# A selective-scan kernel: the scan laid out by channel instead of by channel and state, with a different hand-over between VectorE and GpSimd

## The reference

```python
x_proj = x @ in_proj_w.T + in_proj_b              # 256 -> 512: x_ssm and x_gate
x_conv = silu(depthwise_conv4(x_ssm) + conv_b)
B, C   = split(x_conv @ bc_w.T + bc_b)            # 16 states each, per token
dt     = softplus(x_conv @ dt_w.T + dt_b)         # per token and channel
A      = -exp(A_log)                              # 256 channels x 16 states
h      = h * exp(dt * A) + (dt * B) * x_conv      # scan over 512 tokens
y      = sum_n(h * C) + x_conv * D
z      = (y * silu(x_gate)) @ out_w.T + out_b + x
x1     = layernorm(x + layernorm(z) * ln_g + ln_b)
# experts: top 4 of 8 per token, softmax weights, gated unit of width 512
out    = layernorm(x1 + experts(x1))
```

## Time and profile before

| | us |
|---|---|
| median of 3 runs (1518.12 to 1525.36) | 1522.14 |
| profiled execution, its own time | 1521.88 |
| span of that execution | 1520.1 |
| start of the first scan | 57.6 |
| start of the last scan | 726.3 |
| DVE busy | 1157.5 |
| PE busy | 1073.6 |
| ACT busy | 853.5 |
| POOL busy | 796.4 |

### The profile page before, as it was taken

The page is one execution under the profiler, slowest core; times in us unless marked ns, Lnnn a source line. Parts: engine busy times, 40 slices in busy tenths (PEclk is TensorE's granted clock), DMA queues, the critical chain, the costliest instruction groups (busy, mean ns, idle before and its releaser), DMA issues. The chain is left out here.

```text
span 1520.1 us, 18561 instructions
## 1 busy us (share of the span) xinstructions
PE 1073.6 (71%) x5074; PEld 737.0 (48%) x5074; DVE 1157.5 (76%) x1665; ACT 853.5 (56%) x1353; POOL 796.4 (52%) x519
## 2 busy tenths in 40 slices
PE   6455657383755737351516999999999999999960
PEld 2111222131312213020215888888888888888850
DVE  1688999999998999999444677777777766777753
ACT  2564646455444645532114677777767766777744
POOL 0245557767676776778770444444444444444452
PEclk9786868596876859655557999999999999999995
DMA  1899998888988889786274555666566555565637
GB/s 65 210 275 265 234 273 227 255 253 224 264 243 238 235 253 245 212 265 190 80 258 180 148 147 152 162 166 165 149 150 150 148 150 149 147 155 155 166 62 225
DMA packets 137418, 292.22 MB, mean 192 GB/s; under 512 B 14880, under 2 KB 50464, under 8 KB 132640
## 3 DMA queue, kind: packets, MB, share of 16 engines
q1 hardware_dynamic: 97824, 242.48, 53.1%
q0 software_dynamic: 26880, 36.72, 14.6%
q10 hardware_dynamic: 12672, 12.58, 2.6%
HBM read 232.71 MB, written 59.02 MB: 192 GB/s over the span
## 5 line engine op out<-in xcount | busy, mean ns | idle before, releaser
L956 POOL TENSOR_TENSOR read<-state,c_rep 128x1024 f32<-128x1024 f32 x128 | 301.6, 2357 | 254.1 <-DVE state L796 249.5
L796 DVE TENSOR_TENSOR_SCAN state<-decay,p_bu 128x1024 f32<-128x1024 f32 x128 | 292.3, 2283 | 9.5 <-ACT decay L637 3.5
L1370 POOL DMA_INDIRECT total<-o_v,tok x144 | 267.6, 1858 | 44.1 <-issue 44.0
L637 ACT ACTIVATE decay<-first_wl,scan_rate 128x511 f32<-128x511 f32 x192 | 127.9, 713 | 256.4 <-DVE state L796 227.3
L484 PE MATMUL p_y<-read,small 128*32 128x512 f32 x512 | 96.4, 836 | 217.4 <-POOL read L956 217.4
L1368 POOL TENSOR_TENSOR scrap<-neg_half 128x1 f32<-128x1 f32 x36 | 13.9, 385 | 355.9 <-ACT o_v L1255 353.5
L1232 ACT ACTIVATE gate_v<-p_g,bias 128x512 f32<-128x512 f32 x144 | 98.5, 684 | 97.4 <-PE p_up L1181 97.3
L787 DVE TENSOR_TENSOR p_bu<-first_wh,p_b 128x1024 f32<-128x1024 f32 x96 | 118.0, 1229 | 30.9 <-DMA first_wh<-scan_in 16.2
L484 PEld LDWEIGHTS p_y<-read,small 128*32 128x32 f32 x512 | 11.5, 124 | 267.8 <-POOL read L956 258.1
L1242 ACT ACTIVATE ah<-a_v 128x512 fp32r<-128x512 f32 x144 | 91.2, 633 | 88.2 <-DVE a_v L1316 88.2
L1305 DVE TENSOR_SCALAR up_v<-up_v 128x512 f32<-128x512 f32 x144 | 61.3, 425 | 64.2 <-ACT up_v L1235 64.1
(11 more groups left out here) (200 smaller groups left out, 3017.6 us busy)
## 6 DMA issues: line engine op xcount, KB each, us to landing
first_wl<-scan_in SPq DMA_DIRECT2D x192, 256.0 KB, 4.7
first_wh<-scan_in SPq DMA_DIRECT2D x192, 256.0 KB, 5.7
first_raw<-in_w_experts SPq DMA_DIRECT2D x19, 1668.0 KB, 6.8
raw_w<-in_w_experts SPq DMA_DIRECT2D x18, 1668.0 KB, 6.8
dt_rep<-scan_in SPq DMA_DIRECT2D x64, 256.0 KB, 4.9
u_rep<-scan_in SPq DMA_DIRECT2D x64, 256.0 KB, 5.6
first_rows<-queues SPq DMA_DIRECT2D x19, 544.0 KB, 6.9
xq<-queues SPq DMA_DIRECT2D x18, 544.0 KB, 6.9
```

Of the source, the lines that this page charges most:

```text
L637: act.activation(decay[t % 2][:, i, 1:LEN], dt_rep[t % RING][:, i, 1:LEN], ACT.Exp, scale=rate[:, g:g + 1])\
L796: dve.tensor_tensor_scan(flat(state[t % 4][:, :, :]), flat(decay[t % 2][:, :, :]), p_bu[:, :], 0.0, ALU.mult, ALU.add).then_inc(s_state, 1)
L956: pool.tensor_tensor(read[quad % 2][:, tiles[0]:tiles[0] + 2, :], state[t % 4][:, :, :], c_rep[s.p][:, :].unsqueeze(1).broadcast_to([P, 2, ...
L1370: pool.indirect_dma_start(total, bass.IndirectOffsetOnAxis(ap=tok[t.p][:, a:a + 1], axis=0), o_v[t.p][:, a, :], None, compute_op=ALU.add). ...
```

## The change

- A slot is now one state n of all 256 channels: partition = channel, the two halves of 512 elements are channels 0 to 127 and 128 to 255. `dt` and `u` need no replication: `decays` reads `dt` from SBUF and `u` lies in a PSUM tile `p_u`. Instead B and C (32 rows of 512) go to DRAM and come back spread over all partitions, 1 MB for each two slots (`replicate`); one DMA where there were eight.
- `sum_states` is now, in each slot, two matmuls of 128 columns with the identity as weights, accumulating over 16 slots; the D term is two more matmuls with a diagonal matrix (`skip_w`), in place of `skip_path`. Both halves of `p_y` are one accumulation; the next sequence's starts when `gate` has read it (`s_y`).
- The gate reads PSUM in two instructions, in slot 2 behind the ranking.
- Softplus: two DVE instructions instead of three, one more on ACT, moved to slot 11; dt in slot 13, u in slot 15.
- POOL's read of slot t-1 waits for the product of slot t (`s_bu`), and in slots 2, 5, 11, 12, 13, 15 for the side work named below. The scatters of a slot all stand ahead of that read. The offset of x moves to slot 3; the output bias has `ln_b` taken off and is added by a bfloat16 matmul of three rows.
- The first loads are split: what the input projection needs comes first. The order of A_log and of its biases is set up by small matmuls (`order_rate`, `place_rate`).

```diff
+        def sum_states(s, t):
+            n = SLOTS * s.n + t
+            if t == 0:
+                after(pe, s_y, s.n)
+                for h in range(HALVES):
+                    pe.matmul(p_y[h][:, :], skip_w[:, h, :], xc[s.p][:, h, :], start=True, stop=False)
+            pe.wait_ge(s_read, n + 1)
+            for h in range(HALVES):
+                mm = pe.matmul(p_y[h][:, :], ident[:, :], read[:, t % 4, h, :], start=False, stop=(t == SLOTS - 1))
+            mm.then_inc(s_added, 1)
...
         for r in rounds(pe):
             for t in range(SLOTS):
-                if t in (0, 2) and r.c:
-                    sum_states(r.s.at(-1), QUADS - 2 + t // 2)
-                if t >= 4 and t % 2 == 0 and r.b:
-                    sum_states(r.s, t // 2 - 2)
+                if t < 2 and r.c:
+                    sum_states(r.s.at(-1), SLOTS - 2 + t)
...
                 if r.a and t == 8:
+                    from_xc(r, "bc", BC, 2 * STATE)
...
+                if t >= 2 and r.b:
+                    sum_states(r.s, t - 2)
...
         def softplus(r):
             act.activation(flat(expo[:, :, :]), flat(expo[:, :, :]), ACT.Exp, scale=-1.0).then_inc(s_exp, 1)
+            if r.like == Round.FIRST:
+                rate_exp()
+            act.activation(flat(rest[:, :, :]), flat(expo[:, :, :]), ACT.Identity, bias=1.0).then_inc(s_t, 1)
             act.activation(flat(logp[:, :, :]), flat(expo[:, :, :]), ACT.Ln, bias=1.0).then_inc(s_log, 1)
...
         def decays(s, t):
             after(act, s_state, SLOTS * s.n + t - 1)
+            for h in range(HALVES):
+                act.activation(decay[t % 2][:, h, 1:LEN], dt[s.p][:, h, 1:LEN], ACT.Exp, scale=rate[:, h, t:t + 1])\
                    .then_inc(s_decay, 1)
...
         def softplus_rest(r):
+            dve.wait_ge(s_t, s.n + 1)
+            dve.scalar_tensor_tensor(flat(rest[:, :, :]), flat(rest[:, :, :]), -1.0, flat(expo[:, :, :]),
+                                     ALU.add, ALU.subtract).then_inc(s_rest, 1)
             dve.wait_ge(s_log, s.n + 1)
             dve.tensor_tensor(flat(relu[:, :, :]), flat(relu[:, :, :]), flat(logp[:, :, :]), ALU.add).then_inc(s_sum, 1)
+        def drive(r):
+            after(dve, s_bu, SLOTS * s.n)
+            dve.tensor_tensor(p_u[:, :], flat(dt[s.p][:, :, :]), flat(xc[s.p][:, :, :]), ALU.mult).then_inc(s_u, 1)
...
         def read_state(s, t):
             n = SLOTS * s.n + t
             pool.wait_ge(s_state, n + 1)
+            after(pool, s_added, n - 3)
+            pool.tensor_tensor(read[:, t % 4, :, :], state[t % 4][:, :, :], of_state(t, 1), ALU.mult).then_inc(s_read, 1)
...
+        SCATTERS = {6: (0,), 7: (1,), 8: (2,), 10: (3, 4), 13: (5, 6), 14: (7,), 15: (8,)}
+        def while_scanning(r, t):
+            pool.wait_ge(s_bu, SLOTS * r.s.n + t + 1)
+            if r.d and t == 2:
+                pool.wait_ge(s_rexp, 2 * r.s.at(-2).n + 1)
+            if r.d and t == 5:
+                pool.wait_ge(s_index, r.s.at(-2).n + 1)
+            if r.a and t == 11:
+                pool.wait_ge(s_sum, r.s.at(1).n + 1)
+            if r.c and t == 12:
+                pool.wait_ge(s_residual, r.s.at(-1).n + 1)
+            if r.a and t == 13:
+                pool.wait_ge(s_dt, r.s.at(1).n + 1)
+            if r.a and t == 15:
+                pool.wait_ge(s_u, r.s.at(1).n + 1)
...
+        def replicate(s, pair):
+            if pair == 0:
+                sp.wait_ge(s_put[s.p], 16 * (s.use + 1))
+            after(sp, s_read, SLOTS * s.n + 2 * (pair - RING + 1))
+            rows_of = bc_rows[s.p, 2 * pair:2 * pair + 2, :, :]
+            sp.dma_start(bc[pair % RING][:, :, :, :], rows_of.unsqueeze(0).broadcast_to([P, 2, 2, LEN]))\
+              .then_inc(s_rep[pair % RING], 16)
```

More of the change, by code:

```diff
@@ L72, in blocks @@
         return (["tr0", "tr1", "rt"] * d + ["in0", "in1", "cv0"] * a + ["cnt"] * d + ["cv1"] * a + ["o0", "o1"] * c
-                + ["dt0", "dt1", "bb", "cc", "in2", "in3"] * a)
+                + ["bc", "dt0", "dt1", "in2", "in3"] * a)
     def block(self, name):
[L77 to L80, removed]
+        start = sum(len(Round(Seq(0, i), i).blocks()) for i in range(Round.FIRST, self.like))
+        k = start + self.blocks().index(name)
+        turns = 0 if isinstance(self.s.half, int) else self.s.half - Round.LOOP.start // 2
+        return k % 2, k // 2 + 1 + len(self.blocks()) * turns
 def rounds(eng):
@@ L469, in convolve, with from_xc @@
                 mm.then_inc(bank_full[b], 1)
-        def from_xc(r, name, weight):
+        def from_xc(r, name, at, n):
             bank, done = block(r, name)
-            if name == "dt0":
+            if name == "bc":
                 pe.wait_ge(s_silu, 2 * r.s.at(1).n + 1)
[L475 to L486, removed]
+            product(bank[0:n, :], columns(at, n), lambda k: xc[r.s.at(1).p][:, k, :]).then_inc(done, 1)
+        def sum_states(s, t):
[5 more added lines that the diff above has]
+            pe.wait_ge(s_read, n + 1)
+            for h in range(HALVES):
+                mm = pe.matmul(p_y[h][:, :], ident[:, :], read[:, t % 4, h, :], start=False, stop=(t == SLOTS - 1))
+            mm.then_inc(s_added, 1)
         def project_out(r, b):
@@ L555, in pe_stage1, with rate_rows, rate_exp @@
                     project_out(r, t - 6)
+                if r.like == Round.FIRST and t == 5:
+                    order_rate()
                 if r.a and t == 8:
+                    from_xc(r, "bc", BC, 2 * STATE)
                     for i in range(HALVES):
-                        from_xc(r, f"dt{i}", columns(DT_ + i * P, P))
+                        from_xc(r, f"dt{i}", DT_ + i * P, P)
                 if r.like == Round.FIRST and t == 9:
[L560 to L563, removed]
+                    place_rate()
                 if r.a and t in (10, 11):
                     project(r, t - 8)
+                if t >= 2 and r.b:
+                    if t == 2 and r.like == 0:
+                        pe.wait_ge(s_set_dve, SET_DVE)
+                    sum_states(r.s, t - 2)
     def act_stage1(act):
[L569 to L572, removed]
+        act.wait_ge(s_first, FIRST_SETUP)
+        def rate_rows():
+            act.wait_ge(s_order, 1)
+            for h in range(HALVES):
+                last = act.activation(rate_t[0:STATE, h, :], p_y[h][0:STATE, 0:P], ACT.Copy)
+            last.then_inc(s_set_act, 1)
+        def rate_exp():
+            act.wait_ge(s_order, 2)
+            act.activation(flat(rate[:, :, :]), p_u[:, 0:GROUPS], ACT.Exp).then_inc(s_set_act, 1)
         def store_in(r, m):
@@ L706, in act_stage1 @@
                     store_conv(r, 0)
+                if r.like == Round.FIRST and t == 6:
+                    rate_rows()
                 if r.a and t == 8:
+                    store_bc(r)
                     store_dt(r, 0)
                     store_dt(r, 1)
[L710 to L712 removed]
                 if r.c and t == 9:
@@ L934, in dve_stage1 @@
                     weave(moments(r.s.at(-1), 0))
-                if r.a and t == 10:
+                if r.a and t == (11 if r.b else 10):
                     softplus_rest(r)
-                if r.b and t == 11:
-                    skip_path(r.s, 0)
-                if r.a and t == 11:
+                if r.like == Round.FIRST and t == 11:
+                    negate_rate(dve)
+                if r.a and t == 13:
                     scan_inputs(r)
@@ L942, in dve_stage1 @@
                     residual(r)
+                if r.a and t == SLOTS - 1:
+                    drive(r)
                 if r.b:
@@ L1000, in pool_stage1 @@
             for t in range(SLOTS):
-                if r.d and t in SCATTERS_BEFORE:
-                    scatter(r.s.at(-2), SCATTERS_BEFORE[t])
+                if r.d and t in SCATTERS:
+                    scatter(r.s.at(-2), SCATTERS[t])
+                if r.e and t < 7:
+                    scatter(r.s.at(-3), range(t + 9, t + 10))
+                if r.b:
+                    while_scanning(r, t)
                 if t == 0 and r.c:
```

245 lines of the change are left out of this document (121 added, 124 removed).

## The result

The changed kernel took 1471.99 us (median of 4, 1469.88 to 1474.04) against 1520.13 for the kernel before on the same chip (four executions too): a ratio of 0.968, 95% interval 0.965 to 0.971. The profiled execution took 1474.04 us with a span of 1472.2. I had said 1496.

The account below looks back on a forecast made before the run. VectorE was taken to bound stage 1. Steady rounds -13 us, rounds 0 and 1 -9, round 7 -6, start -2, tail +4: -26 from 1521.9, so 1496 us; own range 1480 to 1514, 8 in 10 1455 to 1545.

Parts of the forecast that it names:

- What bounds it: Stage 1: VectorE bounds, busy 72.4 of 76 us; a microsecond off its instructions is worth one until another engine is late.
- Instructions removed and waits inside durations: VectorE's side work in a steady round: removed instructions and waits for GpSimd recorded as duration, together -7.1 us.
- New wait (1), TensorE before the ranking: Slots 0 to 2: VectorE waits for the logits behind TensorE's sums, 0 to 4 us a round, taken 1.5.
- rival A: PE and ACT keep pace and neither new wait shows: -59 us in all, 1463 us; chance 0.22.
- rival B: PE becomes the bound, where its mean instruction costs over 0.62 us: slower, 1545 us; chance 0.20.
- New wait (2), the decay of slot 10: Slot 10's scan waits for ScalarE's decay, wanted 3.7 us earlier: 0 to 5 us a round, taken 3.
- Rounds 0 and 1: First two rounds of stage 1, without ranking: together 143 us for 152.5, so -9.
- Start: Before the first scan: projection some 4 us earlier, but `place_rate` ahead of the fourth projection; -6 to +3, taken -2.
- Round 7: Last round, without softplus: D term 1.5, ranking 0.7, residual -4.4, wait +0.6, in all -6 us.
- Tail: After the last scan: gate behind ranking, router behind sum 15, 6 to 9 us later, less 2.5 and 2: +4.
- The form of softplus: Softplus's `scalar_tensor_tensor` with two SBUF inputs priced like others; the skill's halved throughput would cost about 1.1 us a round.
- Rival C: The waits only move: POOL's later reads hit other VectorE instructions, the ACT wait eats the rest; 1518 us; chance 0.13.

Follow-up runs that it names:

- e1: Changed kernel without GpSimd's new waits, both for the next slot's product and for the side work: 1506.6 us, ratio 0.992 to the kernel before.
- e2: Changed kernel with GpSimd waiting for the next slot's product but not for the six pieces of side work: 1532.4 us, ratio 1.008.
- e4: Changed kernel with ScalarE making slot 10's decay before its softplus of slot 9 instead of after: 1459.2 us, ratio 0.960.
- e6: Changed kernel with each matmul of `sum_states` done twice, which changes the output: 1553.1 us, ratio 1.022.
- e3: Changed kernel with GpSimd waiting for the six pieces of side work but not for the next slot's product: 1462.7 us, ratio 0.962.
- e10: Changed kernel without the product wait, slot 10's decay before ScalarE's softplus, GpSimd's scale behind VectorE's softplus, slot 10's read behind the second residual: 1439.6 us.
- e7: Kernel before with only GpSimd's new waits added, for the next slot's product and for the side work: 1518.4 us.

## Why the prediction was off

The way was right, and so were most of the mechanisms; the sum fell short by 22 of 48 us. The largest part of that, 13 us, is one term: the time taken off VectorE's instructions, -7.1 us in a steady round, measured -9.7. The next, 8 us, is the start. Windows of rounds 2 to 6, before and after, columns as in the earlier trace rows:

```profile
210.09:650.57 440.48, 256.78 (x825) 106.31 (x825) 414.89 (x436) 228.30 (x326) 310.99 (x193) 0.73 0.87 243
```

```profile
191.06:601.31 410.25, 328.98 (x805) 142.37 (x804) 366.40 (x426) 230.44 (x325) 299.38 (x193) 0.88 0.42 146
```

VectorE's busy time fell by 48.5 us in five rounds, 9.7 in each. Its idle time rose by 3.7 a round, of which waits for ScalarE's decay are 2.9 and waits for TensorE 1.1. That makes the -6.0 of a round where I had -7.1 + 3 + 1.5 = -2.6. By its own steps:

- **What bounds it**: VectorE. Between the changed kernel and `e1` its busy time in rounds 2 to 6 rises by 33.8 us and the rounds by 28.4.
- **Instructions removed and waits inside durations**, -7.1 a steady round: the failed step. The mechanism was right and the size was not. I took each instruction's mean over all eight sequences for its price in a steady round, but the first and the last of them pass while GpSimd has less to do (L773's eight are 1.23, 1.64, 1.62 and five of 4.82). The groups of the kernel before in rounds 2 to 6 alone:

```profile
L773 DVE TENSOR_TENSOR expo<-first_raw,rest 128x1024 f32<-128x1024 f32 x5 | 24.1, 4819 | 0.0
L848 DVE TENSOR_TENSOR z<-z,x 128x1024 f32<-128x1024 f32 x5 | 11.3, 2270 | 0.0
L761 DVE TENSOR_SCALAR rest<-expo 128x1024 f32<-128x1024 f32 x5 | 8.1, 1628 | 0.0
L878 DVE TENSOR_TENSOR ex<-ex,chosen 128x32 f32<-128x32 f32 x5 | 6.6, 1312 | 0.0
L862 DVE TENSOR_TENSOR cmp<-lg 128x256 f32<-128x256 f32 x5 | 6.3, 1262 | 0.2
```

| a steady round, us | predicted | measured in rounds 2 to 6 |
|---|---|---|
| D term | -1.5 | -1.5 |
| softplus | -0.8 | -1.3 (4.05 to 2.76) |
| dt | -2.3 | -3.6 (4.82 to 1.22) |
| second residual | -1.3 | -1.1 (2.27 to 1.22) |
| ranking's first | -0.7 | -0.8 (1.26 to 0.43) |
| weights' first | -0.5 | -1.1 (1.31 to 0.23) |
| gate | 0 | -0.2 |
| small instructions of the statistics | none | -0.6 |

The durations make -10.2; as busy time, which counts the short overlaps of neighbours once, it is -9.7. The largest miss is dt: the earlier trace rows of the prediction had the 4.82 us, the sum used 3.57. The claim under the term, that an instruction of VectorE with two SBUF inputs waits out a running GpSimd instruction, is shown by `e1`, `e2` and `e4`. The Trainium skill says the same (SBUF — State Buffer, "SBUF: two separate sides": the shared pair is held for a whole instruction by whichever started first); the 4.21 and 4.08 us above agree.

- **New wait (1), TensorE before the ranking**, taken 1.5 from 0 to 4: too high, but a small part of the miss. Before the logits it measured 2.0 us in rounds 2 to 6 together, before the places of slot 3, where I had none, 3.3. I had mixed the two clocks by the mean of before, 0.77. At slots 0 to 3 the clock was 1.00 in rounds 3 and 6, where nothing waits, and below it in rounds 2 and 5 (0.92 and 0.70), which have the waits; round 4 has 0.91 and no wait (TensorE alone: length, busy, PEclk, DMA, GB/s, rounds 3 and 5):

```profile
272.65:292.10 19.45, 17.41 (x63) 1.00 0.41 136
437.50:460.54 23.04, 20.62 (x51) 0.70 0.32 109
```

The clock of the long window rose from 0.77 to 0.87, and to 0.98 under `e6`'s load. That goes with the Trainium skill's rule (TensorE: Matmul & The Clock Gate, "The HAM clock gate") that activity releases the throttle, which I had weighed as rival A and held against the tail's 8.00 us at 0.50. The 0.62 us an instruction from which rival B decides was not reached: (65.8 - 11.5) / 112 = 0.48 in rounds 2 to 6. `e6`, with 64 more instructions, would by that working and 0.45 us each need 90.7 us a round; its rounds 2 to 6 are 91.7 to 97.0.

- **New wait (2), the decay of slot 10**, taken 3: 2.85 in round 3, 2.9 a round over rounds 2 to 6. Right, with the right cause.
- **Rounds 0 and 1**, -9 against -9.1: right; the wait for the decay is 3.9 and 4.7 us, taken 4 in each.
- **Start**, taken -2, measured -9.9, and by the spread of the starts above between 5 and 13: the second failed term, 8 of the 22 us. I let `place_rate` cost 32 instructions ahead of the fourth projection and left out what goes from the same stretch: four instructions of B and C, the 3.2 us wait for ScalarE's copy of B, and the first replicas' wait for dt's trip to DRAM, 5.8 us less idle time on VectorE at that place.
- **Round 7**, -6 against -3.5. The residual's instruction was to fall from 5.64 to 1.23 and fell to 3.02, GpSimd's scale being late; in `e3` it takes 1.70, so most of that lateness was the product wait.
- **Tail**, +4 against +4.9: the number is luck. All that I added up lies ahead of the last logits. The first logits do come 5.7 us later (9.7 us after the last scan's start for 4.0), but the last ones come 47.1 us after it, before 47.2. The 4.9 us lie behind them, 2.8 in stages 2 and 3; the cause is open. In `e1` and `e3`, with the same order of gate and router, the tail is 793.7 and 793.3 us, in the kernel before 793.8.
- **The form of softplus**: priced like any other, against the rule of the Trainium skill (Vector Engine (DVE) Microarchitecture Reference, "Points that are easy to get wrong") that two non-bf16 SBUF sources halve its throughput. In `e10`, with nothing in its way, L814 takes 1.22 us for 1024 elements and L817, a plain addition of that size, the same. The rule does not hold for this form here.
- **Rival C**, that the waits only move the blocking, is wrong for the six side waits and right for the product wait: that one alone makes the kernel slower than with none. I had taken all seven as one thing, and my forecast has no price for the first.

## What to carry to other kernels

When two engines block each other for whole instructions, read an instruction's duration against its shortest in the trace; the difference is a wait that no idle column shows. Read it in the rounds that you price and not as a mean over all. To hold one engine back pays only if it waits for exactly the instructions that it would block; a wait that merely lines it up with their start makes them all late. And after removing a wait look at what it covered: the kernel with the decay's new order was 12.8 us faster, but nothing of that was in round 3, until GpSimd's scale was moved too.

## Not expected of the hardware

GpSimd's scale and offset of 128x1024 took 2.49 and 2.35 us before and 2.00 and 1.99 in the changed kernel, while its read of the same size stayed at 2.35. In `e1`, which has the new layout without the waits, they took 2.00 and 1.99; in `e7`, with the old layout and the waits, 2.37 and 2.72. So it goes with the layout and not with the waits; whether it is where `ln_g` and `ln_b` lie in SBUF was not tried.

An instruction with one SBUF input can be held up too. L761 of the kernel before, a `tensor_scalar`, takes 0.69 us at the start, with GpSimd idle, and 0.68 to 0.72 in all its rows in `e7`. In round 3 of the kernel before it took 1.61 and ended 0.56 us after GpSimd's offset (at 346.18). VectorE, then GpSimd:

```profile
345.13 1.61 DVE L761 TENSOR_SCALAR rest<-expo 128x1024 f32<-128x1024 f32 x1
```

```profile
343.83 2.35 POOL L976 TENSOR_TENSOR x<-x,small 128x1024 f32<-128x1024 f32 x1
```
